# Group norm on ScalarE, weight low parts on GpSimd, and v multiplied for four heads side by side

## The chip, the cores and the metric

One Trainium2 chip, of which one core is used: its engines TensorE (PE in the profile), VectorE (DVE), ScalarE (ACT), GpSimd (POOL) and SyncE (SP). The metric is the device time of one execution in microseconds (us), as the median of several runs.

## What is computed

`x` is 16 images of 16x16 positions with 96 channels, so 256 tokens an image, in float32. Cut to what matters:

```python
x = x + conv(group_norm(x))       # 32 groups of 3 channels, mean and variance over an image
t = tokens(x)                     # [16, 256, 96]
t = t + attention(ln(t))          # 6 heads of 16, causal, softmax(k q / sqrt(96)) v, then wproj, bproj
t = t + ffn(ln(t))                # 4 experts 96 -> 384 -> 96, gelu, the 2 best of 4 by a softmax gate

def conv(t):                      # a 1x1 mixture of 5 experts 96 -> 96, the 2 best of 5 by t @ Wg
    gates = softmax(top_2(t @ Wg))
    return leaky_relu(sum(gate_e * (t @ We[e] + be[e])))
```

## The kernel before

**Units.** The work goes in 8 units of two images (512 tokens, four tiles of 128 rows), numbered `@0` to `@7`. A unit runs through: `xt` (transpose of x), `gstat`, `gmean`, `gvar`, `groot` (group norm statistics, in three batches: images 0 and 1, images 2 to 7, images 8 to 15), `xn` (normalised x and its split), `conv` (four tiles of five experts and the gate at once, 486 columns), `gates`, `mix` (the weighted sum of experts), `leaky`, `stats1` and `rstd1` and `norm1` (layer norm), `norm1_t`, `qk`, `v`, `stack` (q and k, split in three bfloat16 parts, laid under each other by DMA), `score` (only for the row maximum), `shift` (minus that maximum, as three bfloat16 rows that a DMA puts under k), `prob` (scores again, transposed, then exp), `pv` (the product with v), `out_t`, `heads_t`, `proj`, `stats2`, `norm2`, `gate2`, `ffn1` (12 pieces of 128 hidden rows), `ffn2` (four experts), `store`.

**Splits.** Products of two float32 values are made of three passes over a high part and a low part (`split_product`, L723 to L727). For weights, ScalarE writes the high part and VectorE the low part: `w_conv` (L1012), `w_qkv` (L1017, L1022), `w_gate` (L1026), `w_w1` (L1030) and `w_b2` (three bfloat16 parts of the last bias, L1035 to L1048). For normalised x, VectorE computes `xn` from `XT` (L1056), ScalarE copies it into `xn_hi` (L611) and GpSimd subtracts into `xn_lo` (L548).

**The order.** `ORDER`, a table of words for each engine, says in which order an engine issues the steps; nothing is reordered at run time. A step waits on semaphores for its inputs and for the buffers it overwrites. Behind `@n:` a PE word has its bank of PSUM. `warm.k` is k matmuls of 128x512 on a constant (L738), whose results nobody reads: they stand where the table's maker expected TensorE to have nothing else to do.

**v.** For each image (`pv.0`, `pv.1`), two groups of three heads (`HG = 3`) are multiplied side by side: head j of a group has its own 32 columns of the array and its own 32 output partitions (L867), `D` columns of v, one of ones for the softmax's sum, and zeros. A group has a pass for the first 128 keys (256 queries) and one for the last 128 keys (128 queries). ScalarE copies 96x512 out (L689), TensorE transposes it back in four pieces of 96x96 an image (L878), and VectorE divides by the sum (L1146, L1150).

```python
for g in range(2):
    for half in range(2):
        for j in range(HG):
            h = HG * g + j
            probs = prob_a[:, b, h, :] if half == 0 else prob_b[:, b, h, :]
            mm = pe.matmul(PS[HS * j:HS * (j + 1), bank("pv", n, index), first_t:(g + 1) * TOKENS],
                           v_augs[n % 2][:, 2 * b + half, h, :], probs, start=half == 0, stop=half == 1, ...)
```

**Constants.** GpSimd writes rows of ones (L542, `pad.0` to `pad.5`) into two `q_stack` buffers, `heads_t`, both `t2_hi` and the second `xn_hi`.

Of the kernel before, what the change touches and what calls it, by code (L numbers as in the profile page):

```python
# [26 lines left out]
HG = 3  # L27
HS = 32
CONV_N = E0 * C + E0 + 1
# [23 lines left out]
        qk.1@1:3 score.0.1@0:5 score.0.2@0:6 score.0.3@0:7 score.0.4@0:2 score.1.0@0:1 score.1.1@0:4 score.1.2@0:0
        conv.1@4:5 norm1_t@2:3 conv.2@4:5 conv.3@4:6 score.1.3@0:7 score.1.4@0:5 warm.19@14:2 shift@0:2 warm.2@15:1
        qk.0@2:1 qk.1@2:4 score.0.0@1:0 score.0.1@1:7 score.0.2@1:5 score.0.3@1:3 prob.0.0@0:6 prob.0.1@0:2
        prob.0.2@0:1 prob.0.3@0:0 score.0.4@1:7 score.1.0@1:4 score.1.1@1:6 score.1.2@1:5 score.1.3@1:2 prob.0.4@0:3
        prob.1.0@0:1 prob.1.1@0:7 prob.1.2@0:0 prob.1.3@0:3 prob.1.4@0:4 score.1.4@1:6 warm.1@16:1 pv.0@0:1
        warm.1@17:7 shift@1:7 out_t.0@0:5 pv.1@0:0 v@2:2 out_t.1@0:3 prob.0.0@1:6 prob.0.1@1:4 prob.0.2@1:1
        prob.0.3@1:7 heads_t@0:5 prob.0.4@1:0 prob.1.0@1:2 prob.1.1@1:3 prob.1.2@1:6 proj@0:5 prob.1.3@1:4
        prob.1.4@1:1 warm.1@18:7 score.0.0@2:7 score.0.1@2:0 score.0.2@2:2 pv.0@1:3 score.0.3@2:6 score.0.4@2:5  # L60
        score.1.0@2:4 pv.1@1:1 score.1.1@2:3 conv.0@5:7 conv.1@5:1 conv.2@5:0 norm2_t@0:2 score.1.2@2:7 score.1.3@2:6
        out_t.0@1:1 out_t.1@1:5 score.1.4@2:4 norm1_t@3:3 gate2@0:2 ffn1.0@0:0 ffn1.1@0:1 ffn1.2@0:5 ffn1.3@0:7
        ffn1.4@0:3 heads_t@1:0 qk.0@3:2 qk.1@3:1 ffn1.5@0:6 ffn1.6@0:5 ffn1.7@0:7 proj@1:4 ffn1.8@0:3 ffn1.9@0:0
        ffn1.10@0:2 ffn1.11@0:6 ffn2.0@0:1 conv.3@5:5 ffn2.1@0:7 conv.0@6:4 shift@2:3 ffn2.2@0:0 conv.1@6:2 conv.2@6:6
        conv.3@6:1 norm2_t@1:5 prob.0.0@2:4 prob.0.1@2:3 prob.0.2@2:7 ffn2.3@0:2 norm1_t@4:6 score.0.0@3:0 v@3:1
        prob.0.3@2:4 prob.0.4@2:3 prob.1.0@2:7 prob.1.1@2:2 prob.1.2@2:1 gate2@1:5 prob.1.3@2:4 prob.1.4@2:0 qk.0@4:3
        pv.0@2:6 ffn1.0@1:7 ffn1.1@1:2 out_t.0@2:1 ffn1.2@1:5 ffn1.3@1:6 pv.1@2:4 v@4:0 ffn2.0@1:7 score.0.1@3:2
# [1160 lines left out]
```

## Time and profile before

| | |
|---|---|
| Median of 3 runs | 370.58 us (370.5 to 370.87) |
| The profiled execution's own time | 369.75 us |
| Its span in the profile | 367.9 us |
| TensorE matmul | 350.3 us busy, 2712 instructions |
| VectorE | 239.5 us busy, 861 instructions |
| ScalarE | 232.7 us busy, 451 instructions |
| GpSimd | 112.3 us busy, 166 instructions |
| Granted TensorE clock | 1.0 of full speed in every slice |

The profile lists for each group of instructions the line, the engine, the tiles written and read, the busy time and the mean of one; the trace gives the same in order of time. TensorE instructions overlap their neighbours, so that the distance between two starts is what one costs, and it is shorter than the printed length of one. A float32 matmul stands in the trace as two instructions.

### The profile page before, as it was taken

To read this page: it belongs to the slowest core of one execution; us is meant where nothing else is said; L and a number is where in the kernel's file an instruction comes from. 1 tells how busy PE (TensorE), PEld (TensorE's weight loads), DVE (VectorE), ACT (ScalarE), POOL (GpSimd) and SP (SyncE) were. 2 spreads that over 40 slices of the span, in tenths; PEclk is the share of its full clock that TensorE was granted. 3 is DMA by queue.
4 is the path that set the end of the run, shared out by engine and by line. 5 is a ranking of instruction groups with operands and counts; after the bars stand their busy time and mean duration, and the time that the engine had idled before them with its cause. 6 is when DMAs were issued, how large, how long until landed. Compare 5 with 4: busy or idle time off the path is not lost.

```text
span 367.9 us, 7639 instructions
## 1 busy us (share of the span) xinstructions
PE 350.3 (95%) x2712; PEld 280.7 (76%) x2712; DVE 239.5 (65%) x861; ACT 232.7 (63%) x451; POOL 112.3 (31%) x166
## 2 busy tenths in 40 slices
...
GB/s 188 149 3 0 0 40 93 59 73 66 67 2 3 127 6 21 53 78 5 3 21 89 45 23 2 120 13 23 11 121 3 21 4 0 23 2 2 23 0 23
DMA packets 23948, 14.76 MB, mean 40 GB/s; under 512 B 14161, under 2 KB 23909, under 8 KB 23910
## 3 DMA queue, kind: packets, MB, share of 16 engines
q1 hardware_dynamic: 22566, 13.09, 17.0%
...
## 4 chain that ended last, share of the span: by engine, by line
PE 71%; DVE 9%; DMA 5%; ACT 5%; issue 4%; SPq 2%; ACTq 2%; POOL 1%; DVEq 0%; POOLq 0%
PE PS L932 21%; PE PS L725 8%; PE PS L727 8%; PE PS L726 8%; PE PS L867 5%; PE PS L738 4%; DMA k_stack<-qk_parts 3%; ACT normed L581 2%; PE PS L849 2%; SPq L469 2%; ACTq L622 2%; DMA k_stack<-shift_t 2%; PE PS L893 2%; PE PS L826 2%; PE PS L780 1%
## 5 line engine op out<-in xcount | busy, mean ns | idle before, releaser
L932 PEld LDWEIGHTS PS<-w_f,hidden 128*128 128x128 f32 x768 | 90.1, 192 | 0.1
L932 PE MATMUL PS<-w_f,hidden 128*128 128x96 f32 x768 | 90.0, 274 | 0.0
L1197 DVE SCALAR_TENSOR_TENSOR res<-PS,weight,res 128x96 f32<-128x96 f32 x128 | 31.7, 310 | 54.8 <-PE PS L932 54.8
L718 ACT ACTIVATE hidden<-PS 128x512 f32<-128x512 f32 x96 | 54.6, 598 | 16.8 <-PE PS L727 14.4
L1127 DVE TENSOR_REDUCE row_max<-PS 128x2 f32<-128x512 f32 (+2 forms) x80 | 46.0, 627 | 6.1 <-PE PS L826 4.3
L738 PE MATMUL PS<-ones_b 128*128 128x512 bf16 x172 | 41.3, 387 | 3.4 <-POOL ones_b L499 3.4
L725 PE MATMUL PS<-t_hi,w_hi 97*128 97x512 f32 x96 | 40.7, 424 | 0.0
L569 POOL TENSOR_SCALAR_AFFINE_SELECT prob_a<-prob_a 128x768 f32<-128x768 f32 x16 | 14.0, 874 | 80.3 <-ACT prob_a L682 80.3
L726 PE MATMUL PS<-t_lo,w_hi 96*128 96x512 f32 x96 | 38.0, 396 | 0.0
L727 PE MATMUL PS<-t_hi,w_lo 97*128 97x512 f32 x96 | 37.9, 395 | 0.0
L1091 DVE SCALAR_TENSOR_TENSOR mixed<-conv_y,weight,mixed 128x96 f32<-128x96 f32 x128 | 34.2, 333 | 1.4 <-ACT mixed L632 1.4
L738 PEld LDWEIGHTS PS<-ones_b 128*128 128x128 bf16 x172 | 16.4, 100 | 21.8 <-issue 5.4
L682 ACT ACTIVATE prob_a<-PS 128x512 f32<-128x512 f32 x48 | 26.2, 599 | 6.5 <-PE PS L849 6.5
L581 ACT ACTIVATE normed<-res,ln_bias,ln_scale 128x96 f32<-128x96 f32 x64 | 24.4, 456 | 4.3 <-POOL ln_bias L530 4.3
L617 ACT ACTIVATE conv_y<-PS 128x486 f32<-128x486 f32 x32 | 18.0, 574 | 10.2 <-PE PS L727 9.2
L560 POOL TENSOR_SCALAR qk_parts<-qk_rest 96x512 bf16<-96x512 f32 x16 | 10.3, 646 | 41.9 <-issue 23.2
L727 PEld LDWEIGHTS PS<-t_hi,w_lo 97*128 97x128 f32 x96 | 18.3, 190 | 4.3
L725 PEld LDWEIGHTS PS<-t_hi,w_hi 97*128 97x128 f32 x96 | 18.2, 190 | 3.9 <-issue 0.8
L718 ACT ACT_TABLE_LOAD x14 | 18.0, 1283 | 4.2 <-PE PS L727 3.8
L569 POOL TENSOR_SCALAR_AFFINE_SELECT prob_b<-prob_b 128x768 f32<-128x768 f32 x16 | 16.1, 1006 | 14.3 <-ACT prob_b L682 14.2
L867 PE MATMUL PS<-prob_a,v_aug 128*32 128x256 f32 x192 | 19.8, 385 | 0.6 <-POOL prob_b L569 0.6
L689 ACT ACTIVATE att_t<-PS 96x512 f32<-96x512 f32 x16 | 9.5, 592 | 17.2 <-PE PS L867 17.2
...
## 6 DMA issues: line engine op xcount, KB each, us to landing
...
```

Source lines behind the costliest of these rows:

```text
L569: pool.affine_select(out=block_, in_=block_, compare_op=ALU.is_ge, fill=0.0, base=0, pattern=[[0, HEADS], [1, P]], channel_multiplier=-1). ...
L581: act.activation(normed[:, which, t, :], rows[:, t, :], ACT.Identity, bias=ln_bias[:, which, t:t + 1], scale=ln_scale[:, which, t:t + 1]). ...
L718: act.activation(hidden[:, m, 0:T * P], PS[:, bank("ffn1", n, index), 0:T * P], ACT.Gelu).then_inc(act_emptied["ffn1"], 1)
L725: pe.matmul(dst, a_hi, b_hi, start=True, stop=False)
L726: pe.matmul(dst, a_hi[0:b_lo.shape[0], :], b_lo, start=False, stop=False)
L727: return pe.matmul(dst, a_lo, b_hi[0:a_lo.shape[0], :], start=False, stop=True)
L738: pe.matmul(PS[:, bank("warm", n, index), :], ones_b[:, :], ones_b[:, :].unsqueeze(1).to_broadcast([P, 4, P]), start=True, stop=True)
L867: mm = pe.matmul(PS[HS * j:HS * (j + 1), bank("pv", n, index), first_t:(g + 1) * TOKENS], v_augs[n % 2][:, 2 * b + half, h, :], probs, sta ...
L932: mm = pe.matmul(PS[:, y, t * C:(t + 1) * C], hidden[:, m, t * P:(t + 1) * P], w2_f[:, m, :], start=False, stop=t == T - 1 and c == CHUNKS ...
L1091: ins = dve.scalar_tensor_tensor(mixed[:, t, :], y, weight0[:, t, e:e + 1], mixed[:, t, :], ALU.mult, ALU.add)
L1127: dve.tensor_reduce(dst, src, AX_X, ALU.max).then_inc(dve_emptied["score"], 1)
L1197: ins = dve.scalar_tensor_tensor(res2[:, t, :], PS[:, y, t * C:(t + 1) * C], weight1[:, t, e:e + 1], res2[:, t, :], ALU.mult, ALU.add).the ...
```

## The change

Five edits:

1. **Group norm.** `xn` on VectorE goes. GpSimd's `groot` also computes `gn_neg` and `gn_bias` = -mean x scale, and ScalarE writes, for each image, `xn_hi` and `xn` straight from `XT` with that scale and bias: four instructions of 96x256 a unit for one of 96x512.
2. **Low parts.** `w_qkv`, `w_w1` and `w_b2` go from VectorE to GpSimd.
3. **Rows of ones.** GpSimd's `pad` steps go. SP issues five DMAs from constant tiles behind the weight loads; the second `xn_hi` row is written by VectorE at the start.
4. **v.** Four heads side by side (`HG = 4`), over the 12 heads of both images of a unit: three rounds, of which `pv.0` has two and `pv.1` one. The copies out are 128x512 and 128x256, the transposes six of 128x128 a unit (`out_t.0` and `out_t.1` now mean the first and second tile of 128 tokens of both images). `pv.0` waits for the probabilities of both images.
5. **The order** of every engine is written anew. It has 134 `warm` matmuls for 172; of them 125 stand ahead of the first `prob` for 169.

Core of the diff:

```diff
-HG = 3
+HG = 4
+ROUNDS = 2 * HEADS // HG
...
-        xn@1 gates.0@0 w_b2.0@0 gates.1@0 w_b2.1@0 mix.1@0 gstat@7 mix.2@0 gmean@2 gates.0@1 gvar@2 xn@2 mix.3@0
+        gates.0@0 gmean@2 gates.1@0 gvar@2 w_gate@0 mix.1@0 mix.2@0 mix.3@0 gates.0@1 mix.4@0 gates.1@1 stats1@0
...
+            sp.wait_ge(const_ready, 3)
+            late = [(q_stack[STACK:STACK + SHIFT, :, :].rearrange("p h (a t) -> p (h a) t", t=P),
+                     ones_b[0:SHIFT, :].unsqueeze(1).to_broadcast([SHIFT, HEADS * TILES, P])) for q_stack in q_stacks]
+            late += [(row[C:C + 1, :].bitcast(F32).rearrange("p (a t) -> p a t", t=P),
+                      ones[0:1, :].unsqueeze(1).to_broadcast([1, TILES, P])) for row in [heads_t] + t2_his]
+            for dst, src in late:
+                sp.dma_start(dst, src).then_inc(late_pads, 16)
...
                     pool.tensor_tensor(gn_veps[:, cols], gn_var[:, cols], eps_t[0:C, cols], ALU.add).then_inc(gn_root, 1)
-                    pool.wait_ge(gn_root, 2 * n + 1)
+                    pool.tensor_scalar(gn_neg[:, cols], gn_mean[:, cols], -1.0, 0.0, ALU.mult, ALU.add).then_inc(gn_root, 1)
+                    pool.wait_ge(gn_root, 4 * n + 1)
                     pool.tensor_tensor(gn_scale[:, cols], gn_veps[:, cols], power_t[0:C, cols], ALU.pow).then_inc(gn_root, 1)
-                elif kind == "pad":
-                    pool.memset(late[index[0]][0], late[index[0]][1]).then_inc(late_pads, 1)
-                    pool.wait_ge(late_pads, index[0] + 1)
+                    pool.wait_ge(gn_root, 4 * n + 3)
+                    pool.tensor_tensor(gn_bias[:, cols], gn_neg[:, cols], gn_scale[:, cols], ALU.mult).then_inc(gn_root, 1)
+                elif kind == "w_qkv":
...
+                elif kind == "w_w1":
+                    pool.wait_ge(w1_split, 1)
+                    pool.tensor_tensor(w1_lo[:, :], w1_f[:, :, :].rearrange("c e h -> c (e h)"),
+                                      w1_hi[:, :].bitcast(F32), ALU.subtract).then_inc(w1_split, 1)
+                elif kind == "w_b2":
...
-                    act.activation(xn_his[n % 2][0:C, 0:T * P], xn[:, 0:T * P], ACT.Copy).then_inc(xn_hi_ready, 1)
+                    for b in range(W):
+                        m = image0 + b
+                        here, image = slice(b * TOKENS, (b + 1) * TOKENS), slice(m * TOKENS, (m + 1) * TOKENS)
+                        act.activation(xn_his[n % 2][0:C, here], XT[:, image], ACT.Identity, bias=gn_bias[:, m:m + 1],
+                                       scale=gn_scale[:, m:m + 1]).then_inc(xn_hi_ready, 1)
+                        act.activation(xn[:, here], XT[:, image], ACT.Identity, bias=gn_bias[:, m:m + 1],
+                                       scale=gn_scale[:, m:m + 1]).then_inc(xn_ready, 1)
...
-                    pe.wait_ge(prob_masked, (2 * (image0 + b) + 2) * UNFUSED)
+                    pe.wait_ge(prob_masked, (2 * (image0 + 1) + 2) * UNFUSED)
...
-                    for g in range(2):
+                    for r in ((0, 1), (2,))[b]:
                         for half in range(2):
                             for j in range(HG):
-                                h = HG * g + j
+                                image, h = divmod(HG * r + j, HEADS)
...
-                    wait_act(pe, "pv", n, index)
-                    for t in range(2):
-                        for g in range(2):
-                            block_ = slice((2 * t + g) * C, (2 * t + g + 1) * C)
-                            mm = pe.transpose(PS[:, bank("out_t", n, index), block_],
-                                              att_t[:, b, g, t * P:(t + 1) * P], ident[0:C, 0:C])
+                    wait_act(pe, "pv", n, (1,))
+                    for r in range(ROUNDS):
+                        mm = pe.transpose(PS[:, bank("out_t", n, index), r * P:(r + 1) * P],
+                                          att_t[:, r, t * P:(t + 1) * P], ident[:, :])
```

What the new order moves is seen in three places. The first is TensorE from the second batch of group means to the first tile of `conv@2`: `ones_b` marks a `warm` matmul, `gn_mv` and `gn_spread` the group averages of images 8 to 15, `conv_hi` a tile of `conv`. Before, with the last passes of `conv@1` ahead:

```order
L725 MATMUL PS<-conv_hi,xn_hi 128x486
L726 MATMUL PS<-conv_lo,xn_hi 128x486
L727 MATMUL PS<-conv_hi,xn_lo 128x486
L738 MATMUL PS<-ones_b 128x512 x10
L756 MATMUL PS<-gn_mv,group_avg 96x8
L738 MATMUL PS<-ones_b 128x512 x6
L760 MATMUL PS<-gn_spread,group_avg 96x8
L738 MATMUL PS<-ones_b 128x512 x44
L725 MATMUL PS<-conv_hi,xn_hi 128x486
```

Now, from the last tile of `conv@0` to the first of `conv@1`, and, behind the "...", from the last of `conv@1` to the first of `conv@2`:

```order
L776 MATMUL PS<-conv_hi,xn_hi 128x486
L777 MATMUL PS<-conv_lo,xn_hi 128x486
L778 MATMUL PS<-conv_hi,xn_lo 128x486
L807 MATMUL PS<-gn_mv,group_avg 96x8
L789 MATMUL PS<-ones_b 128x512 x14
L811 MATMUL PS<-gn_spread,group_avg 96x8
L789 MATMUL PS<-ones_b 128x512 x2
L776 MATMUL PS<-conv_hi,xn_hi 128x486
...
L778 MATMUL PS<-conv_hi,xn_lo 128x486
L789 MATMUL PS<-ones_b 128x512 x27
L776 MATMUL PS<-conv_hi,xn_hi 128x486
```

The averages moved ahead of `conv@1`, and 27 fillers stand between `conv@1` and `conv@2` where 60 stood.

The second is GpSimd behind the roots of the second batch (`power_t` marks a root, `xn_lo` a low part of normalised x). Before, to the first low parts of q:

```order
L540 TENSOR_TENSOR gn_scale<-gn_veps,power_t 96x6
L542 MEMSET xn_hi 1x512
L542 MEMSET q_stack 3x3072
L548 TENSOR_TENSOR xn_lo<-xn,xn_hi 96x512
L542 MEMSET q_stack 3x3072
L542 MEMSET heads_t 1x512
L542 MEMSET t_hi 1x512 x2
L538 TENSOR_TENSOR gn_veps<-gn_var,eps_t 96x8
L540 TENSOR_TENSOR gn_scale<-gn_veps,power_t 96x8
L548 TENSOR_TENSOR xn_lo<-xn,xn_hi 96x512 x2
```

Now, from the same root:

```order
L548 TENSOR_TENSOR gn_bias<-gn_neg,gn_scale 96x6
L552 TENSOR_TENSOR qk_lo<-hidden,qk_hi 96x96 x2
L557 TENSOR_TENSOR wv_lo<-hidden,wv_hi 96x96
L588 TENSOR_TENSOR xn_lo<-xn,xn_hi 96x512
...
L566 CAST hidden<-hidden 65x384
L568 TENSOR_TENSOR hidden<-hidden 65x384
L571 CAST hidden<-hidden 65x384
L573 TENSOR_TENSOR hidden<-hidden 65x384
L588 TENSOR_TENSOR xn_lo<-xn,xn_hi 96x512
...
L561 TENSOR_TENSOR w_lo<-hidden,w_hi 97x1536
```

The memsets are gone, and the low parts of qk, v, b2 and w1 (`hidden` holds their float32 originals) stand between the `xn_lo` steps. The low part of unit 4's x and the root of `rstd1@1` also stand ahead of GpSimd's first `qk` step now; before, they stood behind it.

The third is TensorE at the first `pv`. Before:

```order
L867 MATMUL PS<-prob_a,v_aug 32x256 x3
L867 MATMUL PS<-prob_b,v_aug 32x128 x3
L867 MATMUL PS<-prob_a,v_aug 32x256 x3
L867 MATMUL PS<-prob_b,v_aug 32x128 x3
L738 MATMUL PS<-ones_b 128x512
L834 MATMUL PS<-ident_b,shift_parts 18x128 x4
L878 MATMUL PS<-ident,att_t 128x96 x4
L867 MATMUL PS<-prob_a,v_aug 32x256 x3
L867 MATMUL PS<-prob_b,v_aug 32x128 x3
L867 MATMUL PS<-prob_a,v_aug 32x256 x3
L867 MATMUL PS<-prob_b,v_aug 32x128 x3
```

Now:

```order
L789 MATMUL PS<-ones_b 128x512 x6
L916 MATMUL PS<-prob_a,v_aug 32x256 x4
L916 MATMUL PS<-prob_b,v_aug 32x128 x4
L916 MATMUL PS<-prob_a,v_aug 32x256 x4
L916 MATMUL PS<-prob_b,v_aug 32x128 x4
L916 MATMUL PS<-prob_a,v_aug 32x256 x4
L916 MATMUL PS<-prob_b,v_aug 32x128 x4
```

Four groups of three became three rounds of four, and both halves of the unit stand together, behind six fillers.

## Rows read from the trace of the kernel before

**Rows 1.** The page, part 1: busy time of each engine.

```profile
PE 350.3 (95%) x2712; PEld 280.7 (76%) x2712; DVE 239.5 (65%) x861; ACT 232.7 (63%) x451; POOL 112.3 (31%) x166
```

**Rows 2.** Stretches: length, then busy us (x instructions): PE, PEld, DVE, ACT, POOL.

```profile
0.00:20.00 20.00, 15.54 (x82) 9.94 (x83) 14.57 (x57) 9.94 (x19) 10.22 (x25) 1.00 0.70 155
20.00:60.00 40.00, 36.75 (x176) 20.36 (x175) 36.25 (x128) 19.15 (x46) 21.39 (x22) 1.00 0.15 26
60.00:82.00 22.00, 19.71 (x127) 12.78 (x125) 18.58 (x52) 11.75 (x27) 8.39 (x11) 1.00 0.45 64
82.00:100.00 18.00, 15.85 (x169) 11.38 (x169) 16.87 (x58) 13.10 (x31) 9.03 (x11) 1.00 0.29 68
100.00:340.00 240.00, 238.22 (x1993) 204.12 (x1988) 144.72 (x531) 168.84 (x317) 63.23 (x99) 1.00 0.16 31
```

**Rows 3.** TensorE in order of time: start us, us (the longest run of fillers, the first `prob`).

```profile
30.76 9.66 PE L738 MATMUL PS<-ones_b 128*128 128x512 bf16 x44
81.78 0.82 PE L849 MATMUL PS<-k_stack,q_stack 99*128 99x256 bf16 x6
```

**Rows 4.** VectorE, groups by line from 0 to 75 us: busy us, mean ns.

```profile
L1091 DVE SCALAR_TENSOR_TENSOR mixed<-conv_y,weight,mixed 128x96 f32<-128x96 f32 x52 | 14.0, 332 | 0.0
L1056 DVE TENSOR_SCALAR xn<-XT,gn_mean,gn_scale 96x256 f32<-96x256 f32 x14 | 8.1, 616 | 0.0
```

**Rows 5.** VectorE on tile `hidden` (weight splits) in three stretches.

```profile
15.00:22.00 7.00, 0.69 (x3) 1.00 0.32 64
22.00:37.00 15.00, 5.88 (x7) 1.00 0.00 1
59.00:62.00 3.00, 1.75 (x1) 1.00 0.92 104
```

**Rows 6.** VectorE in order of time.

```profile
16.55 3.20 DVE L1056 TENSOR_SCALAR xn<-XT,gn_mean,gn_scale 96x256 f32<-96x256 f32 x2
36.85 0.73 DVE L1056 TENSOR_SCALAR xn<-XT,gn_mean,gn_scale 96x256 f32<-96x256 f32 x2
```

**Rows 7.** GpSimd in order of time.

```profile
16.91 2.69 POOL L542 MEMSET q_stack<- 3x3072 bf16 x1
20.56 1.26 POOL L548 TENSOR_TENSOR xn_lo<-xn,xn_hi 96x512 fp32r<-96x512 f32 x1 [0.96 <-ACT xn_hi L611]
49.74 0.62 POOL L560 TENSOR_SCALAR qk_parts<-qk_rest 96x512 bf16<-96x512 f32 x1 [8.36 <-DVE qk_rest L1115]
55.67 3.35 POOL L527 TENSOR_TENSOR ln_scale<-ln_var,power_t 128x4 f32<-128x4 f32 x1
65.58 1.06 POOL L527 TENSOR_TENSOR ln_scale<-ln_var,power_t 128x4 f32<-128x4 f32 x1
```

**Rows 8.** GpSimd: a stretch ahead of its first `qk`, and its L542 alone.

```profile
14.60:49.70 35.10, 16.97 (x18) 1.00 0.08 16
0.00:49.00 49.00, 7.53 (x6) 1.00 0.29 64
```

**Rows 9.** TensorE, one `pv` step in order of time.

```profile
99.79 0.63 PE L867 MATMUL PS<-prob_a,v_aug 128*32 128x256 f32 x6
100.25 0.40 PE L867 MATMUL PS<-prob_b,v_aug 128*32 128x128 f32 x6
100.47 0.61 PE L867 MATMUL PS<-prob_a,v_aug 128*32 128x256 f32 x6
```

**Rows 10.** The chain that ended last, in order of time.

```profile
323.17 0.33 PE PS L878 x4
327.40 0.44 PE PS L885 x4
```

**Rows 11.** ScalarE, groups by line and in order of time.

```profile
L689 ACT ACTIVATE att_t<-PS 96x512 f32<-96x512 f32 x16 | 9.5, 592 | 17.2 <-PE PS L867 17.2
L718 ACT ACT_TABLE_LOAD x14 | 18.0, 1283 | 4.2 <-PE PS L727 3.8
43.60 1.53 ACT L581 ACTIVATE normed<-res,ln_bias,ln_scale 128x96 f32<-128x96 f32 x4
85.11 0.38 ACT L682 ACTIVATE prob_b<-PS 128x256 f32<-128x256 f32 x1 [0.84 <-PE PS L853]
```

More of the change, by code:

```diff
@@ L53 @@
[L53 to L67, printed above, removed]
@@ L93 @@
[L93 to L97 removed]
+        gavg.0@1:1 warm.6@3:2 gavg.1@1 conv.0@0:2 conv.1@0:4 conv.2@0:3 conv.3@0:5 gavg.0@2:6 warm.14@4:7 gavg.1@2
@@ new lines @@
+        score.1.0@2:6 score.1.1@2:0 prob.1.3@1:2 prob.1.4@1:7 score.1.2@2:1 score.1.3@2:5 score.1.4@2:3 conv.0@5:2
+        conv.1@5:7 conv.2@5:4 norm2_t@0:6 conv.3@5:0 pv.0@1:2 ffn1.0@0:7 pv.1@1:1 gate2@0:5 norm1_t@3:4 ffn1.1@0:6
+        ffn1.2@0:0 ffn1.3@0:3 out_t.0@1:2 out_t.1@1:1 ffn1.4@0:5 qk.0@3:4 qk.1@3:7 heads_t@1:2 ffn1.5@0:6 ffn1.6@0:1
+        shift@2:0 v@3:3 ffn1.7@0:2 ffn1.8@0:4 ffn1.9@0:5 proj@1:7 ffn1.10@0:0 prob.0.0@2:6 prob.0.1@2:1 prob.0.2@2:2
+        prob.0.3@2:4 prob.0.4@2:5 ffn1.11@0:3 ffn2.0@0:0 prob.1.0@2:7 ffn2.1@0:6 norm2_t@1:1 conv.0@6:2 conv.1@6:4
@@ new lines @@
+        conv.2@6:5 ffn1.0@1:0 ffn1.1@1:7 ffn2.2@0:3 gate2@1:6 ffn2.3@0:2 norm1_t@4:1 conv.3@6:4 prob.1.1@2:5
+        ffn1.2@1:0 ffn1.3@1:7 ffn1.4@1:3 prob.1.2@2:6 score.0.0@3:4 ffn1.5@1:2 ffn2.0@1:5 prob.1.3@2:0 score.0.1@3:7
+        score.0.2@3:1 ffn1.6@1:3 score.0.3@3:4 score.0.4@3:2 prob.1.4@2:6 score.1.0@3:5 qk.0@4:7 score.1.1@3:0
+        ffn2.1@1:1 qk.1@4:4 score.1.2@3:3 score.1.3@3:2 score.1.4@3:5 ffn1.7@1:0 pv.0@2:7 ffn1.8@1:6 pv.1@2:1
+        ffn1.9@1:3 ffn1.10@1:4 out_t.0@2:2 shift@3:5 out_t.1@2:0 ffn2.2@1:7 heads_t@2:6 ffn1.11@1:1 prob.0.0@3:3
@@ new lines @@
+        ffn1.10@2:5 ffn1.11@2:7 heads_t@3:4 ffn2.0@2:0 proj@3:3 shift@4:6 ffn2.1@2:2 ffn2.2@2:1 prob.0.0@4:4
+        norm2_t@3:5 prob.0.1@4:7 ffn2.3@2:0 prob.0.2@4:6 prob.0.3@4:3 prob.0.4@4:2 prob.1.0@4:1 prob.1.1@4:4
+        score.0.0@5:7 score.0.1@5:6 score.0.2@5:0 norm1_t@6:3 prob.1.2@4:5 prob.1.3@4:2 prob.1.4@4:1 score.0.3@5:7
+        ffn1.0@3:6 ffn1.1@3:4 ffn1.2@3:0 score.0.4@5:5 score.1.0@5:3 score.1.1@5:2 score.1.2@5:1 score.1.3@5:7
+        score.1.4@5:6 pv.0@4:5 pv.1@4:4 ffn1.3@3:3 ffn1.4@3:0 shift@5:2 out_t.0@4:1 ffn1.5@3:7 ffn1.6@3:5 ffn1.7@3:6
```

330 lines of the change are left out of this document (159 added, 171 removed).

## The prediction

> **What bounds the kernel now.** I read the busy times first: TensorE works for 350.3 of 367.9 us [rows 1], so 17.6 us of the span are idle on it. Then the stretches [rows 2]: from 100 to 340 us TensorE is busy for 238.2 of 240 us, and no other engine above 169. There only less TensorE work can shorten the span. In the first 100 us it is idle for 12.1 us, and of what it does 40 us are fillers: 169 of the 172 `warm` matmuls stand ahead of the first `prob` at 81.78 us [rows 3]. The head is therefore not bound by TensorE but by what feeds it. There VectorE is the fullest: 36.3 of 40 us from 20 to 60 us, while ScalarE has 19.2 and GpSimd 21.4 [rows 2]. A filler costs 9.66 / 44 = 0.22 us [rows 3]. So two things can be won: a shorter head, of which the fillers are the measure, and TensorE time behind it.
>
> **v, four heads side by side.** In one `pv` step the first group begins at 99.79 us, its second pass at 100.25, and the next group at 100.47 [rows 9]: 0.46 + 0.22 = 0.68 us for the first group. The three heads do run side by side: a transpose of 128 columns costs 0.44 / 4 = 0.11 us [rows 10], so the six instructions of 256 columns in the first pass would take 6 x 0.22 = 1.3 us one behind another, and it takes 0.46. The fourth head is a fourth such column block. Before there are 32 groups (8 units, 2 images, 2 groups), now 24 rounds: 8 fewer, 8 x 0.68 = 5.4 us. I take 5.4. The bounds: a fourth block costs nothing, 5.4 us; or it runs behind the other three (a rival). Transposes back: four pieces of 96x96 take 0.33 us, four of 128x128 take 0.44 [rows 10]. A unit had 8 x 0.083 = 0.66 us and has 6 x 0.11 = 0.66: nothing. ScalarE had two copies of 0.59 us a unit [rows 11] and has one of 0.59 and one of 128x256 at 0.38 [rows 11]: 0.2 us less a unit, on an engine that waits in this part; nothing. VectorE's two divisions stay.
>
> **The head, VectorE's side.** Ahead of `shift@0` it loses seven units of `xn`, 14 instructions, 8.1 us [rows 4]; the low parts of qk and v, 0.7; of b2, 5.9; of w1, 1.75 [rows 5]: 16.4 us. It gains the memset of one row (I count 0.5) and two `mix` steps of four instructions that moved ahead of `shift@0`, 8 x 0.33 = 2.7 us at most [rows 4]. Some 13 us of work are gone from the engine that was fullest: that is the upper bound of what the head can win from this side.
>
> **The head, GpSimd's side.** It loses memsets of 7.5 us [rows 8]. It gains, sized by a two-input step of 96x512 at 1.26 us and a one-input step at 0.62 [rows 7]: w1, 1536 columns, 3 x 1.26 = 3.8; b2, two subtractions of 384 columns at 0.95, two casts and three copies of a row at 0.5, 4.4; qk and v, three of 96 columns at about 0.4, 1.2; the groups' negative means and biases, six of a few values, which the one-input step bounds at 0.62 each; I take 0.2, since they have hardly a column, 1.3. Sum 10.7. From 14.6 to 49.7 us, where its first `qk` begins, it was busy for 17.0 of 35.1 us [rows 8]. Two steps more stand ahead of that `qk` now, an `xn_lo` (1.3) and a root of 1.06 [rows 7] with three small helpers (1.8 in all). So 17.0 - 7.5 + 10.7 + 3.1 = 23.3 us of work, and its first `qk` can begin at 14.6 + 23.3 = 38 us at the earliest, 11.8 us before 49.74 [rows 7]. GpSimd is now nearly full there; the cover that its 18 idle us gave is used up.
>
> **The head, ScalarE's side.** For one copy of 0.63 us, `xn` is four instructions of 96x256 with scale and bias from memory. Four such of 128x96 took 1.53 us [rows 11], and one of 128x256 with a constant scale 0.38: I take 0.48 each and 1.9 us a unit, 1.3 more than before, while VectorE's 0.73 us in front [rows 6] goes: some 0.5 us later for a unit, once. ScalarE has half its time free from 20 to 60 us [rows 2]; this is hidden.
>
> **SP and the constants.** Five small DMAs are issued behind the weight loads, and read only by `heads_t`, `norm2_t` and the first `prob`, tens of us later; SP's next step (`qk.0@0`) waits for GpSimd anyway. Nothing.
>
> **Table loads.** Counting where the ScalarE order goes between exp and gelu, it has 32 loads for 28; at 1.28 us each [rows 11] that is 5.1 us more on an engine with 71 us free from 100 to 340 us [rows 2]. Nothing. The Trainium skill (ScalarE: Activation LUTs, What ACT_TABLE_LOAD costs) states 2.66 us for a switch with its drain: 10.6 us instead of 5.1, as an estimate from that page, which would fit in the same free time; no run here shows yet what a load costs beside its 1.28.
>
> **The sum.** The order has 38 fillers fewer: 38 x 0.22 = 8.3 us that TensorE will not spend. (Ahead of the first `prob` it is 44, or 9.7 us, but four `score` steps went behind it, and six more fillers stand there.) I take this, not VectorE's 13 or GpSimd's 11.8, as the head's gain: a static order can't be faster than its own fillers, and both other sides allow it. With TensorE's idle 17.6 us kept as they are: 369.75 - 5.4 - 8.3 = 356.1 us for the profiled execution. That one stands 0.8 us under the median 370.58, so **357.0 us** on the scale of the medians. The tail (final `ffn2` and store) is the same work.
>
> **Rivals.**
>
> *GpSimd becomes the head's bound.* The rows show the two engines in each other's way: `xn` of unit 1 took 3.20 us for the 0.73 of another unit [rows 6], just beside a 2.69 us memset [rows 7]; and a root of four values took 3.35 us at 55.67 where it took 1.06 at 65.58 [rows 7]. With 23.3 us to do in 23.3 us, each stretch goes straight into the first `qk`. Two or three such stretches (2.3 us each) cost 5 us of the 8.3: 362 us; if all of the head's gain goes, 365.3. The Trainium skill (SBUF — State Buffer, SBUF: two separate sides) has the rule behind this: the pair of ports is locked for a whole instruction and the other engine fully blocks, also where VectorE's step has two inputs in SBUF. By that rule the low parts that moved would still hold up `mix`, whose steps are of this kind; the two rows above agree with it. For it: the new order has these parts just where `mix` runs. Against: it also takes away the two 2.7 us memsets and all the `xn` steps, which were hit. **Chance 0.18.**
>
> *The head wins more.* If waits on TensorE fall along with fillers (12.1 us of idle are there, and VectorE allows 13 us), some 4 us more: 353 us. **0.10.**
>
> *The saturated part begins to wait.* `pv.0` now needs the exps of both images, masked: five exps of 0.38 to 0.59 us [rows 11] and a mask, some 3 us later than before. In most units the order has more TensorE work than this between the last `prob` and `pv.0`. If in three units 2 us stay open: 363 us. **0.05.**
>
> *The fourth head does not run beside the others* (slower than before). If the fourth column block runs behind the three, a round costs 2 x 0.68, and 24 of them 32.6 us instead of 32 x 0.68 = 21.8: 10.9 lost where I count 5.4 won, 357 + 16.3 = 373 us. The change is slower than before only if a fourth block adds over 13.7 / 24 = 0.57 us to a round, five sixths of a round. Nothing in the trace shows a fourth; that three start together speaks against it. **0.03.**
>
> **How the numbers follow.** The forecast has 0.64; its own range is 354 to 360, from VectorE's larger and GpSimd's smaller gain. The overall range, 352 to 364, leaves out the last rival, the far end of the first, and little more. About 0.2% (0.7 us) is what a measurement of this kernel can tell from no change. Faster 0.93: all cases but the last; I keep 0.02 for a near draw, where the whole head gain and some of v's is lost, and 0.05 for slower: the last rival and a mishap of the new order in the saturated part that costs over 14 us.
>
> **What would show it.** In the new profile: 8 `pv` rounds fewer with starts still 0.46 and 0.22 us apart, TensorE busy near 337 us; the first `prob` near 72 us and GpSimd's first `qk` near 40; TensorE idle 15 to 20 us in all and 2 to 3 from 90 to 330. If GpSimd's first `qk` comes after 44 us with hardly any idle time in front, the first rival holds; if rounds are over 1 us apart, the last. If TensorE idles over 6 us in its middle, the order's new waits are the cause and I am wrong on what hides them.

## The result, and the profile after

The changed kernel takes 365.85 us (median of 5 runs, 365.64 to 368.26) against 370.58 us before: a ratio of 0.9872, 95% interval 0.9832 to 0.9913. It is faster, by 4.7 us and not by the 13.6 that I forecast, and it lies outside my range. The profiled execution is the slowest of the five (368.26 us, span 366.5).

The page of the changed kernel: busy times, and from the 40 slices TensorE's busy tenths and its granted clock.

```profile
PE 344.8 (94%) x2658; PEld 279.1 (76%) x2658; DVE 232.5 (63%) x835; ACT 247.5 (68%) x479; POOL 109.3 (30%) x177
...
PE   6789779979999999999999999999999999999996
...
PEclk9989869996999999999999999999999999999999
```

Against [rows 1] TensorE has 5.5 us less and not 13, although 54 instructions are gone (38 fillers and 16 transposes); its idle time is 21.7 us for 17.6. The clock row says why the busy time did not fall: before it was full in every slice.

The windows of the changed kernel (columns as in [rows 2]; the last three are the granted clock, the DMA share and GB/s). The last four are the stretches in which the clock was at half, 1.2 GHz.

```profile
20.00:60.00 40.00, 32.80 (x130) 19.79 (x129) 33.36 (x103) 27.06 (x64) 25.32 (x32) 0.83 0.09 19
60.00:100.00 40.00, 36.04 (x263) 23.39 (x261) 30.38 (x99) 20.04 (x47) 13.02 (x17) 0.91 0.51 72
100.00:340.00 240.00, 238.80 (x2033) 205.46 (x2030) 148.66 (x543) 179.05 (x333) 62.84 (x101) 1.00 0.12 32
24.44:27.85 3.41, 3.41 (x10) 2.45 (x8) 2.49 (x10) 1.79 (x4) 3.19 (x5) 0.50 0.00 0
41.51:44.92 3.41, 3.41 (x9) 1.21 (x8) 3.40 (x2) 1.22 (x3) 3.28 (x2) 0.50 0.01 2
48.33:55.16 6.83, 6.75 (x17) 5.21 (x18) 6.80 (x23) 3.21 (x8) 4.91 (x8) 0.50 0.00 0
82.47:89.29 6.82, 6.02 (x37) 4.70 (x38) 2.77 (x7) 5.40 (x12) 4.63 (x6) 0.50 0.01 2
```

VectorE has 33.4 us of work from 20 to 60 us for 36.3, ScalarE 27.1 for 19.2, GpSimd 25.3 for 21.4: the work moved as the order says. The saturated part, from 100 us, is as full as before, at full clock.

TensorE in order of time (start, us; in brackets how long and for what it waited). These are its four waits of over 1 us behind 20 us. The first two stretches at half clock begin 1.4 and 0.7 us behind the end of such a wait, the other two inside one.

```profile
23.05 0.34 PE L811 MATMUL PS<-gn_spread,group_avg 96*96 96x8 f32 x2 [1.60 <-DVE gn_spread L1052]
...
40.82 0.65 PE L829 MATMUL PS<-ident,normed 128*96 128x128 f32 x4 [2.08 <-ACT normed L621]
...
48.41 0.71 PE L776 MATMUL PS<-t_hi,qk_hi 96*96 96x512 f32 x1 [2.67 <-DVE t_lo L1115]
...
83.27 1.46 PE L898 MATMUL PS<-k_stack,q_stack 99*128 99x256 bf16 x6 [2.85 <-DMA k_stack<-shift_t]
```

The last is the first `prob`: at 83.27 us, 1.5 us later than before [rows 3], with 38 fillers fewer in the whole order. So the head won nothing. What the kernel gained lies behind it: 366.54 - 83.27 = 283.3 us from there to the end, where before it was 367.9 - 81.8 = 286.1.

The wait of 2.67 us leads to the cause. VectorE and then GpSimd of the changed kernel, around 40 us:

```profile
39.37 4.30 DVE L1012 TENSOR_TENSOR beats<-conv_y 128x100 f32<-128x100 f32 x1 [0.49 <-ACT conv_y L666]
43.59 1.32 DVE L1013 TENSOR_TENSOR beats<-conv_y 128x100 f32<-128x100 f32 x1
44.94 0.26 DVE L1015 TENSOR_TENSOR beats<-beats,before 128x100 f32<-128x100 f32 x1
...
47.59 0.68 DVE L1115 TENSOR_TENSOR t_lo<-PS,t_hi 96x512 fp32r<-96x512 f32 x1
```

```profile
38.90 1.26 POOL L588 TENSOR_TENSOR xn_lo<-xn,xn_hi 96x512 fp32r<-96x512 f32 x1
40.12 3.43 POOL L561 TENSOR_TENSOR w_lo<-hidden,w_hi 97x1536 fp32r<-97x1536 f32 x1
43.50 1.29 POOL L588 TENSOR_TENSOR xn_lo<-xn,xn_hi 96x512 fp32r<-96x512 f32 x1
...
51.81 0.69 POOL L600 TENSOR_SCALAR qk_parts<-qk_rest 96x512 bf16<-96x512 f32 x1
```

The comparisons of `gates.0@2` (128x100, two inputs in SBUF) take 0.26 us elsewhere. Here the first takes 4.30 and the second 1.32: the first ends 0.1 us behind the low part of w1, the second 0.1 us behind the `xn_lo` that follows it. Everything behind it on VectorE is 5 us late, `t_lo` of unit 0 among it, for which `qk.0@0` on TensorE waits, and GpSimd's own first `qk` behind that: 51.81 us, where I had expected 40 and before it was 49.74 [rows 7].

The first wait, 1.60 us, has a smaller hold behind it: VectorE's `gn_spread` takes 1.25 us at 21.75 where the steps of its size in front of it take 0.16, beside an `xn_lo` of 1.26 us at 21.72 on GpSimd.

So two theories stood beside each other. **The hold**: GpSimd's steps hold VectorE's, and the worst one costs the head 4 to 5 us. **The clock**: the waits let TensorE's clock fall, 20.5 us at half. A rival to both: the new head is worth nothing by itself, and v's 5.4 us are all there is.

### The profile page after: what moved, and what is told of

Read it like the earlier page. It is cut to its first block, busy times and chain, and to the rows that moved or that the text cites. A ratio compares the mean times of both kernels' runs of the same rounds, so it can differ in the third digit from the quotient of the medians.

```text
span 366.5 us, 7539 instructions
## 1 busy us (share of the span) xinstructions
PE 344.8 (94%) x2658; PEld 279.1 (76%) x2658; DVE 232.5 (63%) x835; ACT 247.5 (68%) x479; POOL 109.3 (30%) x177
## 4 chain that ended last, share of the span: by engine, by line
PE 63%; issue 10%; SPq 8%; DVE 6%; DMA 5%; ACT 5%; POOL 3%; ACTq 0%; DVEq 0%; POOLq 0%
PE PS L979 18%; PE PS L776 8%; SPq L480 8%; PE PS L777 7%; PE PS L778 7%; DMA k_stack<-shift_t 4%; PE PS L898 3%; PE PS L789 3%; PE PS L916 2%; PE PS L940 2%; PE PS L829 2%; PE PS L902 2%; DVE beats L1012 1%; PE PS L875 1%; PE PS L973 1%
## 5 line engine op out<-in xcount | busy, mean ns | idle before, releaser
L1098 DVE SCALAR_TENSOR_TENSOR mixed<-conv_y,weight,mixed 128x96 f32<-128x96 f32 x128 | 37.3, 359 | 0.9 <-ACT mixed L681 0.9
L789 PE MATMUL PS<-ones_b 128*128 128x512 bf16 x134 | 34.2, 404 | 3.4 <-POOL ones_b L510 3.4
L769 ACT ACT_TABLE_LOAD x16 | 20.5, 1283 | 11.4 <-PE PS L778 11.1
L789 PEld LDWEIGHTS PS<-ones_b 128*128 128x128 bf16 x134 | 13.1, 104 | 18.8 <-issue 6.7
L777 PEld LDWEIGHTS PS<-t_lo,w_hi 96*128 96x128 f32 x96 | 18.2, 189 | 2.6
L898 PE MATMUL PS<-k_stack,q_stack 99*128 99x256 bf16 x96 | 16.0, 292 | 3.9 <-DMA k_stack<-shift_t 3.9
L603 POOL TENSOR_TENSOR qk_parts<-qk_rest,qk_parts 96x512 bf16<-96x512 f32 x16 | 18.8, 1174 | 2.4
```

The costliest lines, as they stand in the source:

```text
L769: act.activation(hidden[:, m, 0:T * P], PS[:, bank("ffn1", n, index), 0:T * P], ACT.Gelu).then_inc(act_emptied["ffn1"], 1)
L777: pe.matmul(dst, a_hi[0:b_lo.shape[0], :], b_lo, start=False, stop=False)
L789: pe.matmul(PS[:, bank("warm", n, index), :], ones_b[:, :], ones_b[:, :].unsqueeze(1).to_broadcast([P, 4, P]), start=True, stop=True)
L898: mm = pe.matmul(dst[:, j * TOKENS:(j + 1) * TOKENS], q[0:STACK + SHIFT, 2 * k + j, t0:t0 + P], kk[0:STACK + SHIFT, 2 * k + j, t0:t0 + TOK ...
L1098: ins = dve.scalar_tensor_tensor(mixed[:, t, :], y, weight0[:, t, e:e + 1], mixed[:, t, :], ALU.mult, ALU.add)
```

## The experiments

All have 6 or 12 timed executions; "ratio" is against the kernel before on the same chip, with its 95% interval. The last two columns split the span of the profiled execution at the first `prob`. They are single executions, and these differ already at the first group average (8.2 to 9.3 us), so less than 1 us in "first `prob`" is no difference.

| kernel | median us | ratio | first `prob` | from there |
|---|---|---|---|---|
| before (370.9 to 371.5 beside the experiments) | 370.6 | 1 | 81.8 | 286.1 |
| the change | 365.9 | 0.987 [0.983, 0.991] | 83.3 | 283.3 |
| v_three | 371.5 | 0.997 [0.993, 1.001] | 83.1 | 287.7 |
| w1_late | 361.8 | 0.976 [0.972, 0.979] | 78.0 | 280.7 |
| fill | 365.0 | 0.982 [0.978, 0.987] | 80.0 | 280.2 |
| b_few_fill | 369.3 | 0.996 [0.993, 0.998] | 82.3 | 285.8 |
| lows_dve | 365.3 | 0.985 [0.980, 0.989] | 81.1 | 282.4 |
| xn_dve | 366.1 | 0.987 [0.982, 0.991] | 82.9 | 281.8 |
| w1_fill | 359.4 | 0.967 [0.963, 0.971] | 76.7 | 280.6 |
| w1_b2_late | 361.6 | 0.972 [0.967, 0.976] | 78.3 | 283.6 |
| w1_pieces | 366.1 | 0.985 [0.980, 0.990] | 81.9 | 282.6 |
| fill_w1_dve | 361.1 | 0.971 [0.967, 0.975] | 78.0 | 280.8 |
| fill_xn_dve | 365.3 | 0.981 [0.977, 0.985] | 82.2 | 281.7 |
| fill_v_three | 364.0 | 0.978 [0.975, 0.982] | 76.5 | 284.8 |

### v_three: the v step alone put back

```diff
-HG = 4
+HG = 3
# att_t, inv_sum and the steps pv and out_t of the kernel before
```

> The changed kernel with the v step alone put back: three heads side by side, two rounds an image, four 96-row transposes an image, everything else and every order as changed. Theory A (the whole gain is the v step, 8 rounds x 0.68 us = 5.4, and the new head gives nothing): 365.9 + 5.4 = 371.3, no gain left over the kernel before (370.6). Theory B (the head gives some of its 8 us and something else eats it late): between 366 and 369, the first prob at 83 us all the same, and the loss would have to be found behind 90 us. First prob unchanged at 83.3 us in either.

371.5 us, no measurable gain over the kernel before. The head is the same to 0.2 us, and the 4.4 us are all behind the first `prob`. Theory A: in the changed kernel, as it runs, the new head gives nothing, and v gives all of the gain. Four of v_three's twelve executions take 368.1 to 368.6 us, with mean clocks of 0.981 to 0.991 where the profiled one has 0.970: where the clock falls less the head gives something.

### w1_late: GpSimd's low part of w1 eight steps later

```diff
 GPSIMD:
-... rstd1@0 xn@3 w_w1@0 xn@4 rstd1@1 qk.0@0 qk.1@0 xn@5 rstd1@2 qk.0@1 qk.1@1 xn@6 ...
+... rstd1@0 xn@3 xn@4 rstd1@1 qk.0@0 qk.1@0 xn@5 rstd1@2 qk.0@1 qk.1@1 w_w1@0 xn@6 ...
```

> The changed kernel with GpSimd's low part of w1 (3.43 us at 40.12, beside which VectorE's comparison of 128x100 took 4.30 us and not 0.25) moved behind GpSimd's qk.1@1, where VectorE reads scores from PSUM. Theory A (GpSimd's two-input step holds VectorE's two-input steps, and VectorE sets when qk.0@0 starts): the comparison at 39 us takes 0.3 us, t_lo comes some 4 us earlier, near 43.5, and so do qk.0@0 (48.4 to some 44.5) and the first prob (83.3 to 79 or 80); time 362 to 363. Theory B (qk.0@0 is held by ScalarE's copy t_hi, or what VectorE gains is eaten at the next wait, such as the stack transfers): first prob 82 to 83.3, time 365 to 366. Theory C (the same 4 us stretch turns up wherever the step stands, since it holds whatever VectorE does beside it): VectorE's steps near 70 us stretch instead, time 365 to 367.

361.8 us, 4.1 less than the change, and the first `prob` at 78.0. VectorE of w1_late in order of time, first where the hold was, then where the step went:

```profile
38.84 0.91 DVE L1012 TENSOR_TENSOR beats<-conv_y 128x100 f32<-128x100 f32 x1 [0.48 <-ACT conv_y L666]
39.67 0.25 DVE L1013 TENSOR_TENSOR beats<-conv_y 128x100 f32<-128x100 f32 x1
...
43.77 0.68 DVE L1115 TENSOR_TENSOR t_lo<-PS,t_hi 96x512 fp32r<-96x512 f32 x1
...
65.58 4.93 DVE L1134 TENSOR_REDUCE row_max<-PS 128x2 f32<-128x256 f32 x9
70.55 0.91 DVE L1140 TENSOR_SCALAR shift_parts<-row_max 128x24 bf16<-128x24 f32 x1
71.49 1.19 DVE L1142 SCALAR_TENSOR_TENSOR shift_rest<-row_max,shift_parts 128x24 f32<-128x24 f32 x1
```

GpSimd of w1_late in the same stretch:

```profile
67.99 3.43 POOL L561 TENSOR_TENSOR w_lo<-hidden,w_hi 97x1536 fp32r<-97x1536 f32 x1
71.39 1.26 POOL L588 TENSOR_TENSOR xn_lo<-xn,xn_hi 96x512 fp32r<-96x512 f32 x1
```

The same 3.43 us lie beside VectorE's reductions from PSUM, nine in 4.93 us, 0.55 each, and these don't stretch. The two small steps behind them, whose inputs are in SBUF, are still held, 2.1 us together for 0.2 each when free. So Theory A, with a little of C. The first comparison still takes 0.91 us beside an `xn_lo`. The other kernels with the group norm on ScalarE have a hold of this kind too, though not always on this step: in w1_fill a `mix` step takes 1.32 us at 37.28.

No filler was added here, and yet this profiled execution keeps the full clock but for its last microseconds. TensorE of w1_late, the steps that waited in the changed kernel:

```profile
23.64 0.33 PE L811 MATMUL PS<-gn_spread,group_avg 96*96 96x8 f32 x2 [1.60 <-DVE gn_spread L1052]
...
40.30 0.64 PE L829 MATMUL PS<-ident,normed 128*96 128x128 f32 x4 [2.52 <-ACT normed L621]
...
44.60 0.45 PE L776 MATMUL PS<-t_hi,qk_hi 96*96 96x512 f32 x1 [1.07 <-DVE t_lo L1115]
...
77.97 0.83 PE L898 MATMUL PS<-k_stack,q_stack 99*128 99x256 bf16 x6 [1.41 <-DMA k_stack<-shift_t]
```

Only the last two waits are shorter, 1.07 us for 2.67 and 1.41 for 2.85; the first is as long as it was and the second longer. So the hold made part of the waits, and why the clock stayed up behind 1.60 and 2.52 us here and not in the changed kernel isn't shown. Four of w1_late's six executions show mean clocks of 0.991 to 0.998, two 1.0.

### fill: 40 more fillers where TensorE waited

```diff
 PE:
-warm.14@4:7 gavg.1@2    warm.10@7:7 norm1_t@0:7    warm.12@8:0 qk.0@0:0    qk.1@2:2 prob.0.0@0:4
+warm.21@4:7 gavg.1@2    warm.19@7:7 norm1_t@0:7    warm.24@8:0 qk.0@0:0    qk.1@2:2 warm.12@15:4 prob.0.0@0:4
```

> The changed kernel with 40 more fillers at the four waits after which the granted clock was 0.5: 7 ahead of gavg.1@2, 9 ahead of norm1_t@0, 12 ahead of qk.0@0 and 12 in a new group ahead of the first prob (each group as long as the wait it stands in, at 0.22 us a filler). Theory A (the idle TensorE lets the clock fall, and 20.5 us at 1.2 GHz cost the path 3 to 6 us, most of it in 82.47 to 89.29): the clock stays at 1.0 and the time is 361 to 364. Theory B (the clock's fall is harmless, because the head waits for other engines and catches up): clock 1.0, time 365 to 366.5. Theory C (the fillers push the work): more than 367. No part of the result changes.

The profiled execution holds the clock at 1.0 and takes 362.0 us, with the first `prob` at 80.0 and 280.2 us from there. The hold is still there, on two `mix` steps (4.72 us at 37.58, 1.32 at 42.45). So in this execution a held clock is worth 3 us on either side of the first `prob`. But the other five show mean clocks of 0.990 to 0.995 and 363.0 to 366.2 us: these fillers alone don't hold it reliably. The median, 365.0, doesn't stand clear of the change's, since the two intervals overlap.

### b_few_fill: 38 fillers taken from the kernel before

```diff
 PE:
-warm.44@8:4 conv.0@2:4
+warm.6@8:4 conv.0@2:4
```

> The kernel before with 38 fillers fewer in one place: 6 and not 44 in the group ahead of conv.0@2. Theory A (the step of my prediction taken literally: the path is as long as TensorE is busy plus 17.6 us, so each filler fewer is 0.22 us less): 370.6 - 8.4 = 362.2. Theory B (fillers only stand in a wait whose end other engines set): 370.6, with 8.4 us more of idle TensorE, ended by GpSimd's xn_lo or ScalarE, the first prob at 81.8 as before. Theory C (B, and the idle lets the clock fall to 0.5 for some us): 371 to 375, with rows of granted clock below 1.0 behind the gap.

This is the test of the step that my sum rests on. 369.3 us: 1.6 less, where a literal reading asks for 8.4. TensorE of this kernel in order of time, the group that is left and the step behind it:

```profile
31.80 1.46 PE L738 MATMUL PS<-ones_b 128*128 128x512 bf16 x6
37.41 0.78 PE L725 MATMUL PS<-conv_hi,xn_hi 97*128 97x486 f32 x1 [4.15 <-POOL xn_lo L548]
37.98 0.61 PE L726 MATMUL PS<-conv_lo,xn_hi 97*128 97x486 f32 x1
38.38 0.61 PE L727 MATMUL PS<-conv_hi,xn_lo 96*128 96x486 f32 x1
```

Of the 8.4 us of fillers half was cover for a wait that GpSimd ends (4.15 us). The rest let `conv` of unit 2 start at 37.4 and not at 40.1, and that bought little: the clock is at half for 6.8 us from 36.6, inside the gap (`conv` passes 0.4 us apart, not 0.22), and the first `prob` comes at 82.3, not at 81.8. This execution began late: its first `conv` pass is at 15.90 us for 14.87 before, so that from there to the first `prob` it is 0.5 us shorter. It is also the longest of the twelve (369.8 us), so the median's 1.6 us stand beside some 1 us in the profiles. Theory B with C's clock, without its price: 8.4 us of fillers bought 1 to 2.

### lows_dve and xn_dve: one half of the new head put back

```diff
# lows_dve
-GPSIMD: w_qkv@0 w_b2.0@0 w_b2.1@0 w_b2.2@0 w_w1@0
+VECTOR: gstat@6 w_qkv@0    gates.0@0 w_b2.0@0    gates.1@0 w_b2.1@0    mix.4@0 w_b2.2@0    gates.0@3 w_w1@0
# xn_dve
-SCALAR xn: four scaled copies out of XT a unit
+VECTOR: gstat@3 xn@0   gstat@6 xn@1   gvar@2 xn@2   mix.4@0 xn@3   gates.0@2 xn@4   mix.1@2 xn@5 ...
```

> The changed kernel with all low parts (w_qkv, w_b2, w_w1) back on VectorE at the places that they had before; group norm stays on ScalarE, v stays four heads wide. Against the changed kernel (365.9). Theory A (my prediction's: these steps on VectorE are worth 8.3 us of its path): the head is longer by some of that, the first prob 85 us or later and the time 368 or more. Theory B (on GpSimd the one step w_w1 cost VectorE 4 us by holding it, so that the move gave nothing, and taking it back costs nothing): first prob 80 to 83, time 363 to 366, and no VectorE comparison above 1 us between 36 and 46 us.

> The changed kernel with the group norm's scaling (xn) back on VectorE and one ScalarE copy a unit as before; the low parts stay on GpSimd. The places of VectorE's xn steps are chosen by hand near those of the kernel before. Theory A (the group norm on ScalarE is a real part of the gain: 8.1 us of VectorE ahead of the first shift): first prob 86 us or later, time 368 to 371. Theory B (VectorE does not set the head, ScalarE's queue does, and 1.1 us a unit less on ScalarE helps): first prob 81 to 83, time 364 to 366.

365.3 and 366.1 us: neither is told from the change. For lows_dve that is Theory B: no comparison from 36 to 46 us takes over 0.63 us, and the low parts on GpSimd gave VectorE room and took as much by the hold. Its mean clocks are 0.965 to 0.986, so a gain of a few us by the clock could be hidden in it. xn_dve is inconclusive: it still has the hold (a `mix` instruction of 4.72 us at 39.22) and the clock at half for 13.7 us. Putting the group norm back costs nothing while something else is late.

### w1_fill: both remedies, and the best of all

w1_late with `warm.20@4`, `warm.20@7`, `warm.18@8` and a new `warm.6@15:4` ahead of `prob.0.0@0`: 28 fillers more, sized by w1_late's waits.

> w1_late (GpSimd's low part of w1 behind qk.1@1) and 28 fillers more at the waits that its trace shows: 6 ahead of gavg.1@2 (wait 1.6 us), 10 ahead of norm1_t@0 (2.5), 6 ahead of qk.0@0 (1.4), 6 ahead of the first prob (1.4). Theory A (w1_late's executions of 360.4 to 363.0 differ by clock that falls in some): the executions come closer together at a mean clock of 1.0, median 360 to 361. Theory B (those differences are transfers, not clock): median 361.5 to 362.5 with the same spread, though the clock is 1.0. Theory C (the fillers push the work behind them): over 362.5.

359.4 us (358.3 to 360.4 in six executions, mean clock 0.995 to 1.0), 11.7 us below the kernel before on the same chip and 6.5 below the change (7.4 by the two ratios). Windows of w1_fill, then TensorE ahead of the first `prob`:

```profile
20.00:60.00 40.00, 38.10 (x187) 22.77 (x185) 37.15 (x128) 30.23 (x73) 23.72 (x35) 1.00 0.17 31
...
100.00:340.00 240.00, 239.49 (x2014) 206.91 (x2013) 143.18 (x530) 179.23 (x329) 57.77 (x94) 1.00 0.14 31
```

```profile
75.14 1.47 PE L789 MATMUL PS<-ones_b 128*128 128x512 bf16 x6
76.74 0.83 PE L898 MATMUL PS<-k_stack,q_stack 99*128 99x256 bf16 x6
```

Against the rows at half clock above, `prob` takes 0.83 and not 1.46 us for six, and no wait stands in front of it. 162 fillers are in this order, 28 more than in the change, and its first `prob` comes 6.5 us earlier. The execution of fill shown above, with the hold and the full clock, stands half-way, at 80.0: of the 6.5 us some 3 go with the clock and some 3 with the hold.

### w1_b2_late and w1_pieces: what holds, and for how long

```diff
# w1_b2_late: GPSIMD, behind w1_late's place
+... qk.1@1 w_w1@0 w_b2.0@0 w_b2.1@0 w_b2.2@0 xn@6 ...
# w1_pieces: the change, same place
-pool.tensor_tensor(w1_lo[:, :], ...)
+for e in range(E1): pool.tensor_tensor(w1_lo[:, e * HID:(e + 1) * HID], ...)
```

> w1_late and b2's seven low steps moved behind it on GpSimd as well. Theory A (every two-input step on GpSimd holds VectorE: b2's at 23 to 30 us stretch the comparisons and masks there, such as the chosen step of 1.72 us at 29.50 in w1_late): VectorE gains 1.5 to 2 us before 32 us, first prob 76 to 77, time 360 to 361. Theory B (b2's steps were in VectorE's waits, or GpSimd is late for the probs' masks behind them): first prob 78, time 361.8, or later where GpSimd's prob masks come behind.

361.6 us, as w1_late, and the first `prob` at 78.3: by time and first `prob` Theory B. But A's mechanism is there: in w1_late a comparison took 0.69 us at 27.73 and the small step `chosen` 1.71 at 29.50, beside b2's steps and an `xn_lo`; here they take 0.26 and 0.18. All six executions have lower mean clocks (0.980 to 0.991, w1_late's 0.991 to 1.0), and the profiled one is at half clock for 6.8 us from 16.6 and from 61.0; what the missing holds gave may have gone there. Its 2.9 us more behind the first `prob` are TensorE's idle time: 1.7 us from 78 to 85 and 1.4 from 200 to 250, where w1_late has 0.3 and none.

> The changed kernel with GpSimd's low part of w1 cut into four steps of 97x384 at the same place, nothing else moved. Theory A (a two-input step of VectorE can't run beside one of GpSimd and gets its turn between two of them): no VectorE step at 37 to 44 us takes over 1.3 us, VectorE gains 3 us of the 4 there, first prob 79 to 80.5, time 362 to 363.5. Theory B (VectorE only comes when GpSimd has no step waiting): the stretch stays near 4 us in one or more steps, time 365 to 366, and only the place of the step helps.

366.1 us, no gain. VectorE and then GpSimd of w1_pieces:

```profile
38.92 3.77 DVE L1014 TENSOR_TENSOR beats<-conv_y 128x100 f32<-128x100 f32 x1 [0.49 <-ACT conv_y L668]
42.61 1.05 DVE L1015 TENSOR_TENSOR beats<-conv_y 128x100 f32<-128x100 f32 x1
43.70 1.21 DVE L1017 TENSOR_TENSOR beats<-beats,before 128x100 f32<-128x100 f32 x1
```

```profile
38.45 1.26 POOL L590 TENSOR_TENSOR xn_lo<-xn,xn_hi 96x512 fp32r<-96x512 f32 x1
39.67 3.88 POOL L563 TENSOR_TENSOR w_lo<-hidden,w_hi 97x384 fp32r<-97x384 f32 x4
43.51 1.28 POOL L590 TENSOR_TENSOR xn_lo<-xn,xn_hi 96x512 fp32r<-96x512 f32 x1
```

The pieces take 0.97 us each, so they end near 40.6, 41.6, 42.6 and 43.55. VectorE's step waited through `xn_lo` and three pieces and got its turn near 42.6; the next two waited for one piece or step each. Theory B in time, though VectorE did get in ahead of the last piece: between steps that stand close together on GpSimd it mostly doesn't. Shorter steps were no remedy here; a place beside VectorE's reads of PSUM was.

### fill_w1_dve, fill_xn_dve, fill_v_three: each part's worth with the head in order

w1_fill with one part put back as above: w1's low part on VectorE, the group norm on VectorE, v with three heads.

> w1_fill (359.4) with w1's low part on VectorE after gates.0@3, as in the kernel before, and not on GpSimd. VectorE then does 1.75 us more ahead of the first scores, where it is late. Theory A (VectorE sets the head between 48 and 70 us): first prob 1 to 2 us later than w1_fill's 76.7, time 360.5 to 361.5. Theory B (there the ScalarE queue with its transfers sets it): same time, 359 to 360.

> w1_fill (359.4, first prob 76.7) with the group norm's scaling back on VectorE, xn steps at hand-chosen places near those of the kernel before, one ScalarE copy a unit. With the 4 us hold gone and the clock held, this is the group norm's own worth. Theory A (VectorE's 8.1 us ahead of the first shift are on the path): first prob 80 to 84, time 363 to 367. Theory B (they lie in VectorE's waits, and the group norm on ScalarE gives nothing): first prob 76 to 78, time 359 to 361.

> w1_fill (359.4) with the v step of the kernel before: three heads side by side and eight transposes of 96 rows. The clock is held here, so this is the v step's own worth. Theory A (8 rounds x 0.68 us on a busy TensorE): 359.4 + 5.4 = 364.8, first prob unchanged at 76.7, all of it behind 87 us. Theory B (the transposes of 128 rows, ScalarE's longer copies of 128 partitions or the later start of v, which now waits for both images, take part of it back): 361.5 to 363.5.

Taken as differences of the ratios times 371 us, since these three ran on another chip than w1_fill, where the kernel before took 0.4 us more: w1 off VectorE is worth 1.5 us (0.971 for 0.967; the intervals overlap, and the first `prob` is 1.3 us later, 0.3 of it ahead of the first `conv`), the group norm on ScalarE 5.1 (0.981), and v 4.1 (0.978). Theory A for the group norm, though part of its 5.1 may be clock, which was at half for 6.8 us from 61.9 in its profiled execution (mean clocks of its executions 0.978 to 0.994, w1_fill's 0.995 to 1.0). In the profiles v's 4.2 us are all behind the first `prob` (284.8 against 280.6, both at full clock there): 364.0 us lies between Theory A's 364.8 and Theory B's upper end.

## Why the prediction was wrong

**v: right in kind, 5.4 us for a measured 4.1.** TensorE, one `pv` step of the changed kernel, beside [rows 9]:

```profile
93.07 0.64 PE L916 MATMUL PS<-prob_a,v_aug 128*32 128x256 f32 x8
93.52 0.40 PE L916 MATMUL PS<-prob_b,v_aug 128*32 128x128 f32 x8
93.74 0.61 PE L916 MATMUL PS<-prob_a,v_aug 128*32 128x256 f32 x8
```

Starts 0.45 and 0.22 us apart, with eight instructions for six: the fourth head costs nothing, and the rival on it falls. Summed over all units, from the first instruction to the one behind the step, `pv` takes 22.25 us in fill_v_three and 17.12 in w1_fill, 5.1 less, and the transposes 5.5 and 5.4, as I had said. So v's own price was right to 0.3 us, and about 1 us of it doesn't reach the end of the kernel; where that goes isn't traced.

**"I take this, not VectorE's 13 or GpSimd's 11.8, as the head's gain": the step that failed.** Two things were wrong with it. First its reading: a filler is cover that somebody sized, and its number follows from a guess at the waits. Taking 38 out of the kernel before moved the first `prob` by +0.5 us, in an execution that began 1.0 us late, and the time by -1.6; the best kernel has 28 more of them than the change and is 6.5 us faster. Its argument, that an order can't be faster than its own fillers, bounds the time from below only, and I used it as an estimate. Second its size: with hold and clock mended, the head's gain is 81.8 - 76.7 = 5.0 us, not 8.3, though VectorE lost 13.

**"TensorE's idle 17.6 us kept as they are", at full clock: the term that was missing.** Idle was 21.7, and 20.5 us ran at 1.2 GHz. The account of the profiled spans: forecast 367.9 - 5.4 - 8.3 = 354.2, measured 366.5, 12.3 more. Ahead of the first `prob` it is 83.3 - (81.8 - 8.3) = 9.8: 3.3 from the gain's size, and 6.5 from hold and clock (83.3 against w1_fill's 76.7; fill, with the hold and the full clock, at 80.0). Behind it, 283.3 - (286.1 - 5.4) = 2.6, which is the stretch at half clock from 82.47, whose 6.0 us of work cost half of that, 3.0, more than they should. The profile of before had the clock at 1.0 throughout, and I took that as given; no rival asked what the order's new waits would do to it. Nor is the kernel before always at full clock: beside the experiments 13 of its 45 executions had mean clocks of 0.984 to 0.991 and took 373.2 to 375.2 us.

**The first rival (GpSimd as the head's bound, 0.18) had the right mechanism and the wrong price.** Its far end, "if all of the head's gain goes, 365.3", is nearly what was measured, but only in part by its own cause: the clock took about as much as the hold. "Two or three such stretches (2.3 us each)" became one of 4.0 and one of 1.0 us, end to end, beside a step that I had sized at 3.8 us and that took 3.43. GpSimd itself was not full: it idled 5.08 us ahead of its second layer-norm root at 49.87, since it waited for the VectorE that it had held; so of the rival's sign, a first `qk` after 44 us with hardly any idle time in front, only the first half came (51.81 us). I had the Trainium skill's rule (SBUF — State Buffer, SBUF: two separate sides) at hand and let "it also takes away the two 2.7 us memsets" outweigh it. Of the two rows that I set beside it neither shows GpSimd holding a VectorE step with two inputs: in one the held step has one input, in the other it is GpSimd's that is held. By that rule the comparison at 39.37, two inputs in SBUF beside a GpSimd step that reads SBUF, is blocked until that step ends. The trace agrees that it is blocked, and goes past the rule: `xn_lo` ended at 40.16, and the comparison took 4.30 us for 0.26, since the 3.43 us step that followed at once held it too.

**What held.** Transposes, ScalarE's copies for v, SP's constants and the saturated part cost what I said: at held clock the part behind the first `prob` is 280.2 to 280.8 us where I forecast 280.7. ScalarE's `xn` is 1.97 us a unit for my 1.9, and hidden; its table loads are 32 for 28, as counted, at the same 1.28 us.
